# Four column tiles of 32 in place of two of 64 for the values and the probability products of a decoder's self and cross attention

## The chip, the cores and the metric

The kernel runs on one core of a Trainium2 chip. The metric is the device time of one execution in microseconds; the kernel before takes 1644.26 us, the median of three runs (1642.93 to 1644.7). All times of the profile are microseconds from the start of the span unless ns is written. Engines: TensorE has two rows in a profile, PE for matmuls and PEld for the loads of stationary operands; VectorE is DVE, ScalarE is ACT, GpSimd is POOL, SyncE (which issues DMAs) is SP.

## The reference, cut to what matters

Two decoder layers over x and a context, both of shape (64, 64, 128), fp32: 64 sequences of 64 tokens. The change lies in the first two of six steps, a self and a cross attention with 16 heads of 8 dimensions. Cut to its core, with x the tokens that ask and kv the tokens that are read (x itself, then the context):

```python
q, k, v = x @ Wq, kv @ Wk, kv @ Wv          # 128 -> 16 heads of 8
s = einsum('bhnd,bhmd->bhnm', q, k) / sqrt(8)   # cross: causal mask
attn = softmax(s, axis=-1)
out = einsum('bhnm,bhmd->bhnd', attn, v)
x = layernorm(x + (out @ Wo + b))
```

After them come a feed-forward layer, a differential attention, a latent attention with routing, and a mixture of experts. They are untouched by the change.

## The kernel before, in words

**Tiling.** The 64 sequences are taken in 32 pairs, so that 128 tokens fill the partitions. Self attention over the 32 pairs and cross attention over the same 32 run as one pipeline of 64 items in the class `LowHeads`. Each engine has its own method (`tensor`, `scalar`, `vector`, `gpsimd`, `sync`), and each of them is a list of slots: slot i does a piece of item i and pieces of its neighbours. `slots` writes slots -1 to 7 out, then runs a loop of five iterations of four slots (`Fori(2, 7)`), writes 28 to 35 out, runs six iterations of four slots (`Fori(9, 15)`), and writes the rest out. The flags in the code mean: `on(d)`, item i + d exists; `cr(d)`, it is a cross item.

**One slot of TensorE** (the order is written out by hand; every engine takes its instructions in program order, and the engines meet only at semaphores):
- `scores(i)`, L342: eight matmuls for item i, each with 32 rows (four heads) and 64 stationary columns (queries of one sequence); the keys, spread by head on the diagonal (`k_diag`), move, 256 columns. It waits for `qT_ready`, `kd_ready` and `sub_done`: the score banks must have been read. A cross item adds mask matmuls in bf16 (L353).
- L379: transposes of the tokens of item i + 1.
- `turn(i, par, 0)`, L366: four transposes of the probabilities of item i - 1, heads 0 to 7.
- L388: transpose of the normed output of item i - 2.
- L397: keys of item i + 1. Then `turn(.., 1)`, the other four transposes. L403: the output projection of item i - 2. L408: queries of item i + 1.
- L414, the values of item i + 1: the stationary operand is the tokens of one sequence (64 columns), the moving one the value weights of the even or of the odd heads (`wv`, 128 columns with zeros between). Even heads land in partitions 0 to 63 of the bank, odd ones in 64 to 127. Four matmuls.
- L428, the products of the probabilities with the values, item i - 1: for each of 8 pairs of heads and each of 2 sequences, 64 queries are the stationary columns; 18 columns move (8 + 8 values and two columns of ones for the sums of the probabilities). Sixteen matmuls. Afterwards `av_done` rises.

An fp32 matmul shows in the trace as two passes, each with its own load and matmul record (a transpose as one); so L414 has 8 records a slot and L428 has 32.

**The other engines.** VectorE takes, for item i, the maximum of the scores of heads 0 to 7 (L515) and subtracts it (L520, which raises `sub_done`), and the same for heads 8 to 15; between the two it adds the output projection of item i - 2 to z (L554, waits for L403), afterwards it takes the statistics of z (L559). At the start of the slot it takes the reciprocal of the sums (L530, waits for `av_done`) and norms the output (L538). ScalarE copies tokens (L452), the transposed output (L458), keys (L463), transposed probabilities (L469, twice), queries (L474) and values (L484, waits for `av_done`), and takes the exponentials (L444, twice). GpSimd spreads the keys (L599, 1.04 us) and does the rest of the norm. SyncE issues the loads and stores.

**PSUM.** The values lie in bank 2, which holds a half of the transposed probabilities at another time of the slot; the products lie in bank 1.

Of the kernel before, what the change touches and what calls it, by code (L numbers as in the profile page):

```python
# [29 lines left out]
P = 128  # L30
B, S, D = 64, 64, 128
# [14 lines left out]
def wait(eng, sem, count):  # L46

    if not isinstance(count, int) or count > 0:
        eng.wait_ge(sem, count)
# [145 lines left out]
class LowHeads:  # L195
# [121 lines left out]
    def tensor(self, pe, between=None):  # L317
        core, nc = self.core, self.nc
        ps_qk, ps_tail = core.bank[0], core.bank[1]
        ps_t = [core.bank[2], core.bank[3]]  # L320
        ps_v, ps_x = ps_t[0], ps_t[1]
        ps_s = [core.bank[4 + g] for g in range(4)]
        ps_o = ps_tail[:, 0:VW * H0 // 2].rearrange("p (g e) -> p g e", e=VW)
        ps_oT, ps_out = ps_tail[:, 2 * P:3 * P], ps_tail[:, 3 * P:4 * P]

        def cross_weights():

            pe.wait_ge(self.loads[1].loaded, self.loads[1].all)
            for n in range(4):
                last = nc.tensor.transpose(ps_tail[:, n * P:(n + 1) * P], self.loads[1].tile["raw"][:, n, :],  # L330
                                           core.ident[:, :])
            last.then_inc(self.flat_done, 1)

        def scores(i, par, cross):

            wait(pe, self.qT_ready, i + 1)
            wait(pe, self.kd_ready, i + 1)
            wait(pe, self.sub_done, 2 * i)
            for g in range(4):
                at = slice(32 * g, 32 * (g + 1))  # L340
                for b in range(2):
                    last = nc.tensor.matmul(  # L342
                        ps_s[g][b * S:(b + 1) * S, 0:4 * S].rearrange("p (h t) -> p h t", h=4),
                        self.qT[at, par, b * S:(b + 1) * S], self.k_diag[at, par, :, b * S:(b + 1) * S],
                        start=True, stop=not cross)
                if not cross and g % 2:
                    last.then_inc(self.s_done, 1)
            if cross:
                for half in range(2):
                    for g in range(4):  # L350
                        at = slice(32 * g, 32 * (g + 1))
                        cols = slice(half * S // 2, (half + 1) * S // 2)
                        last = nc.tensor.matmul(  # L353
                            ps_s[g][:, 0:4 * S].rearrange("p (h t) -> p h t", h=4)[:, :, cols],
                            self.masks.left[at, half, :, :, :].rearrange("p b f l -> p (b f l)"),
                            self.masks.right[at, half, None, :].to_broadcast([S // 2, 4, S // 2]), start=False,
                            stop=half == 1)
                        if half and g % 2:
                            last.then_inc(self.s_done, 1)

        def turn(i, par, c):

            wait(pe, self.exp_done, 2 * i - 1 + c)
            for hp in range(4):
                src = self.prob[:, 1 - par, 8 * c + 2 * hp:8 * c + 2 * hp + 2, :].rearrange("p h t -> p (h t)")
                last = nc.tensor.transpose(ps_t[c][:, hp * P:(hp + 1) * P], src, core.ident[:, :])  # L366
            last.then_inc(self.t_done, 1)

        def slot(i, k, par, on, cr):
            if on(0):  # L370
                scores(i, par, cr(0))
            if on(1):

                cross = cr(1)
                wait(pe, self.x_loaded[1 - par], 32 * (k + par + 1) - 8 * NPAIR if cross else 16 * (k + par + 1))
                wait(pe, self.pT_ready, 2 * i - 2)
                wait(pe, self.xT_ready, i + 1)
                for m in range(2 if cross else 1):
                    last = nc.tensor.transpose(ps_x[:, m * P:(m + 1) * P], self.x_t[:, 1 - par, m, :], core.ident[:, :])  # L379
                last.then_inc(self.xt_done, 1)  # L380
            if on(-1):

                wait(pe, self.v_ready, i + 1 if on(0) else NI)
                turn(i, par, 0)
            if on(-2):

                wait(pe, self.onorm_done, i - 1)
                nc.tensor.transpose(ps_oT, self.o_norm[:, par, :], core.ident[:, :]).then_inc(self.ot_done, 1)  # L388
            if on(1):

                w = int(cr(1))
                if isinstance(i, int) and i == -1:
                    pe.wait_ge(self.w_copied, 5)
                wait(pe, self.xT_ready, i + 2)
                wait(pe, self.qT_ready, i + 1)
                kv = self.xT[:, w, :]
                nc.tensor.matmul(ps_qk[:, P:2 * P], self.wk[:, w, :], kv, start=True, stop=True).then_inc(self.k_done, 1)  # L397
            if on(-1):
                turn(i, par, 1)
            if on(-2):  # L400

                wait(pe, self.oT_ready, i - 1)
                nc.tensor.matmul(ps_out, self.oT[:, :], self.wo[:, int(cr(-2)), :], start=True, stop=True)\  # L403
                    .then_inc(self.out_done, 1)
            if on(1):

                wait(pe, self.kT_ready, i + 2)
                nc.tensor.matmul(ps_qk[:, 0:P], self.wq[:, w, :], self.xT[:, 0, :], start=True, stop=True)\  # L408
                    .then_inc(self.q_done, 1)

                wait(pe, self.pT_ready, 2 * i - 1)
                for b in range(2):
                    for odd in range(2):
                        last = nc.tensor.matmul(ps_v[odd * S:(odd + 1) * S, b * P:(b + 1) * P],  # L414
                                                kv[:, b * S:(b + 1) * S], self.wv[:, w, odd, :], start=True, stop=True)
                last.then_inc(self.v_done, 1)
            if isinstance(i, int) and i == -1:
                cross_weights()
            if on(-1):

                wait(pe, self.z_done, i - 1)
                if isinstance(i, int) and i == 1:
                    pe.wait_ge(self.w_copied, 10)
                for hp in range(8):
                    if hp % 4 == 0:
                        wait(pe, self.pT_ready, 2 * i - 1 + hp // 4)
                    for b in range(2):
                        last = nc.tensor.matmul(ps_o[b * S:(b + 1) * S, hp, :], self.probT[:, hp, b * S:(b + 1) * S],  # L428
                                                self.v_blk[:, 1 - par, b, hp, :], start=True, stop=True)
                last.then_inc(self.av_done, 1)  # L430

        pe.wait_ge(self.consts.ident_done, 1)
        self.slots(pe, slot, between)

    def scalar(self, act, between=None):
# [2188 lines left out]
```

## Time and profile before

| | us |
|---|---|
| median of the runs (1642.93, 1644.26, 1644.7) | 1644.26 |
| span of the profiled execution | 1642.7 |
| PE busy | 1577.1 (96%) |
| PEld busy | 1321.5 (80%) |
| DVE busy | 1227.7 (75%) |
| ACT busy | 914.9 (56%) |
| POOL busy | 676.4 (41%) |

The profiled execution's own time is given by its span alone; the lowest run, 1642.93, lies 0.2 above it and the median 1.6. Busy times of PE are sums over overlapping, modelled matmuls: an engine that shows work at each moment need not be the limit. What a line of a timeline means: start, length from the first start to the last end of merged instructions, engine, line of the code, operation, tile written and tiles read, shape, number, and in brackets the idle time of the engine before it with what ended it. A shape as 128*64 128x18 is that of a matmul: 128 rows and 64 columns of the stationary operand, 18 moving columns. "Granted clock" (PEclk) is the TensorE clock that the throttle let through, as a share of 2.4 GHz.

### The profile page before, as it was taken

To read this page: it belongs to the slowest core of one execution; us is meant where nothing else is said; L and a number is where in the kernel's file an instruction comes from. 1 tells how busy PE (TensorE), PEld (TensorE's weight loads), DVE (VectorE), ACT (ScalarE), POOL (GpSimd) and SP (SyncE) were. 2 spreads that over 40 slices of the span, in tenths; PEclk is the share of its full clock that TensorE was granted. 3 is DMA by queue.
4 is the path that set the end of the run, shared out by engine and by line. 5 is a ranking of instruction groups with operands and counts; after the bars stand their busy time and mean duration, and the time that the engine had idled before them with its cause. 6 is when DMAs were issued, how large, how long until landed. Compare 5 with 4: busy or idle time off the path is not lost. (4 is left out here: it accounts for less than half of the span.)

```text
span 1642.7 us, 51985 instructions
## 1 busy us (share of the span) xinstructions
PE 1577.1 (96%) x18084; PEld 1321.5 (80%) x18084; DVE 1227.7 (75%) x3513; ACT 914.9 (56%) x2620; POOL 676.4 (41%) x1068
## 2 busy tenths in 40 slices
PE   7999999999999999999999999899999999999795
PEld 5887788787777777777777777699999999999664
DVE  6889888677776777777777677478888888888664
ACT  5777777643544445544444545566666666666251
POOL 3666665411233333333333333234444444444345
PEclk9999999999999999999999999999999999999997
DMA  3214212121221000000001010122122122122231
GB/s 98 74 44 120 72 56 58 44 58 46 61 58 27 26 26 26 26 26 26 26 26 29 27 30 22 30 58 63 44 63 61 43 63 61 44 63 59 77 116 32
DMA packets 157654, 82.30 MB, mean 50 GB/s; under 512 B 17641, under 2 KB 153115, under 8 KB 157568
## 3 DMA queue, kind: packets, MB, share of 16 engines
q1 hardware_dynamic: 154800, 77.68, 17.7%
q0 software_dynamic: 2048, 3.15, 0.6%
q8 instruction: 52, 0.85, 0.2%
q10 hardware_dynamic: 720, 0.33, 0.1%
q14 instruction: 34, 0.28, 0.1%
HBM read 61.03 MB, written 21.27 MB: 50 GB/s over the span
## 5 line engine op out<-in xcount | busy, mean ns | idle before, releaser
L1489 PE MATMUL bank<-diff_xT,diff_w_score 128*128 128x128 f32 x2048 | 256.4, 278 | 0.7 <-ACT diff_xT L1606 0.7
L1489 PEld LDWEIGHTS bank<-diff_xT,diff_w_score 128*128 128x128 f32 x2048 | 238.7, 192 | 22.4 <-issue 20.2
L1613 ACT ACTIVATE diff_keys<-bank 128x512 f32<-128x512 f32 x256 | 152.3, 595 | 161.7 <-PE bank L1489 161.7
L2092 ACT ACTIVATE lat_prob<-bank,lat_neg_max 128x128 f32<-128x128 f32 x512 | 180.7, 367 | 89.9 <-DVE lat_neg_max L2247 89.4
L1803 POOL TENSOR_TENSOR diff_prob<-diff_prob,diff_inv_sum 128x512 f32<-128x512 f32 x64 | 67.1, 1049 | 369.4 <-DVE diff_inv_sum L1706 369.4
L2309 POOL TENSOR_TENSOR lat_prob<-lat_prob,lat_inv_sum 128x512 f32<-128x512 f32 x128 | 133.4, 1042 | 147.6 <-DVE lat_inv_sum L2229 146.6
L1983 PE MATMUL bank<-lat_catT,lat_w_score 128*128 128x128 f32 x1024 | 137.9, 278 | 3.2 <-issue 2.6
L2015 PE MATMUL bank<-lat_catT,lat_query 128*128 128x128 f32 x1024 | 138.7, 278 | 2.3 <-ACT lat_query L2103 2.1
L2003 PE MATMUL bank<-lat_w_vo,lat_ctxT 128*128 128x128 f32 x1024 | 130.3, 275 | 1.1 <-ACT lat_ctxT L2115 1.1
L1983 PEld LDWEIGHTS bank<-lat_catT,lat_w_score 128*128 128x128 f32 x1024 | 124.4, 192 | 4.8 <-issue 3.9
L2015 PEld LDWEIGHTS bank<-lat_catT,lat_query 128*128 128x128 f32 x1024 | 124.5, 192 | 4.7 <-ACT lat_query L2103 3.7
L2003 PEld LDWEIGHTS bank<-lat_w_vo,lat_ctxT 128*128 128x128 f32 x1024 | 122.1, 192 | 1.3 <-ACT lat_ctxT L2115 1.3
L1993 PE MATMUL bank<-lat_probT,lat_c_rep 32*128 32x256 f32 x2048 | 119.5, 380 | 2.4 <-DVE lat_z L2217 2.4
L1993 PEld LDWEIGHTS bank<-lat_probT,lat_c_rep 32*128 32x128 f32 x2048 | 102.0, 185 | 11.0 <-issue 2.6
L2103 ACT ACTIVATE lat_query<-bank 128x512 f32<-128x512 f32 x128 | 76.7, 599 | 57.5 <-PE bank L1983 56.8
L599 POOL TENSOR_TENSOR low_k_diag<-low_kT,low_head_of 128x512 f32<-128x512 f32 x64 | 66.5, 1040 | 100.0 <-ACT low_kT L463 100.0
L1517 PE MATMUL bank<-diff_mix,diff_raw_qkv 128*64 128x128 f32 x1024 | 105.1, 278 | 1.0 <-DVE diff_mix L1732 1.0
L2223 DVE STREAM_TRANSPOSE lat_probT<-lat_prob 128x512 f32<-128x512 f32 x128 | 90.8, 709 | 19.5 <-POOL lat_prob L2309 12.0
L2092 ACT ACTIVATION_READ_ACCUMULATOR lat_prob<-bank,lat_neg_max 128x1 f32 x512 | 104.9, 205 | 0.0
L1766 DVE STREAM_TRANSPOSE diff_probT<-diff_prob 128x768 f32<-128x768 f32 x64 | 62.6, 979 | 56.4 <-POOL diff_prob L1807 54.7
L1517 PE MATMUL bank<-diff_mix,diff_wv 128*64 128x128 f32 x1024 | 102.7, 273 | 0.0
L1732 DVE COPY diff_mix<-bank 128x512 f32<-128x512 f32 x128 | 82.5, 686 | 24.2 <-PE bank L1504 24.2
(274 smaller groups left out, 3684.3 us busy)
## 6 DMA issues: line engine op xcount, KB each, us to landing
lat_c_rep<-cat SPq DMA_DIRECT2D x128, 128.0 KB
stage<-low_y SPq DMA_DIRECT2D x64, 64.0 KB, 1.6
diff_x_rep<-stage SPq DMA_DIRECT2D x128, 32.0 KB, 1.8
lat_c_t<-cat SPq DMA_DIRECT2D x32, 128.0 KB, 2.2
exp_w<-in_L_ffn_w_dram SPq DMA_DIRECT2D x16, 256.0 KB
expert_rows<-latw_zeros SPq DMA_DIRECT2D x4, 548.0 KB, 5.6
exp_rows<-expert_rows SPq DMA_DIRECT2D x8, 274.0 KB
low_x_t<-in_x_dram SPq DMA_DIRECT2D x32, 64.0 KB, 1.9
```

Of the source, the lines that this page charges most:

```text
L1489: last = nc.tensor.matmul(ring[(k + d) % 2][:, j * P:(j + 1) * P], w_score[:, H1 * (k // 2) + HS * d + 4 * (k % 2) + j, :], xT[:, :], star ...
L1517: last = nc.tensor.matmul(ring[d][par * HD1:(par + 1) * HD1, t * P:(t + 1) * P] .rearrange("p (b f l) -> p b f l", b=2, f=2), w, tokens, s ...
L1613: nc.scalar.activation(keys[:, k // 2, 4 * (k % 2):4 * (k % 2) + 4, :].rearrange("p h t -> p (h t)"), ring[(k + d) % 2][:, :], ACT.Copy).t ...
L1732: nc.vector.tensor_copy(mix[:, q % 2::2, :, q // 2, :], ps_mix[q][:, :].rearrange("p (f h l) -> p f h l", f=2, h=HS))\
L1983: last = nc.tensor.matmul(ps_g[:, h * P:(h + 1) * P].rearrange("p (b s) -> p b s", b=2), w_score[:, 4 * c + h, :], catT[:, par, :, S:T], s ...
L1993: last = nc.tensor.matmul(ps_c[r][:, 256 * b:256 * (b + 1)].rearrange("p (c h s) -> p c h s", c=4, h=2), c_rep[at, b, tq, :], moving, star ...
L2003: last = nc.tensor.matmul(ps_o, ctxT[:, 2 * m + odd, :, :].rearrange("p b s -> p (b s)"), w_vo[:, odd, m, :], start=(n == 0), stop=(n == 15))
L2015: last = nc.tensor.matmul(ps[:, m * T:(m + 1) * T], query[:, c % 2, b, 2 * hp:2 * hp + 2, :].rearrange("p h s -> p (h s)"), catT[:, par, b ...
L2092: last = nc.scalar.activation(prob[:, q, m, :], ps_s[q][:, m * T:(m + 1) * T], ACT.Exp, bias=neg_max[:, q, m:m + 1], accum_out=row_sum[:, ...
L2103: nc.scalar.activation(query[:, c % 2, :, :, :], ps_g[:, :].rearrange("p (h b s) -> p b h s", h=4, b=2), ACT.Copy)\
L2223: nc.vector.transpose(probT[:, par if c > 1 else 1 - par, (c + 2) % 4, :, :] .rearrange("p m t -> p (m t)"), prob[:, q, :, :].rearrange("p ...
L2309: nc.gpsimd.tensor_tensor(prob[:, q, :, :], prob[:, q, :, :], inv_sum[:, q, :, None].to_broadcast([P, 4, T]), ALU.mult)\
```

## The change

The values of a sequence were one matmul for each of even and odd heads, with 64 stationary columns (its tokens); they become two with 32 columns, each on a column tile of 32. The products of a pair of heads were one matmul for each sequence, with 64 stationary columns (its queries); they become two with 32 columns. What lands in which partition of the bank is the same, as are the waits, the semaphores and the work of the other engines. L is 32.

```diff
@@ tensor()
+        L = S // 2
@@ values
                 for b in range(2):
-                    for odd in range(2):
-                        last = nc.tensor.matmul(ps_v[odd * S:(odd + 1) * S, b * P:(b + 1) * P],
-                                                kv[:, b * S:(b + 1) * S], self.wv[:, w, odd, :], start=True, stop=True)
+                    for n in range(4):
+                        odd, at = n // 2, b * S + L * (n % 2)
+                        last = nc.tensor.matmul(ps_v[L * n:L * (n + 1), b * P:(b + 1) * P], kv[:, at:at + L],
+                                                self.wv[:, w, odd, :], start=True, stop=True)
@@ products
-                    for b in range(2):
-                        last = nc.tensor.matmul(ps_o[b * S:(b + 1) * S, hp, :], self.probT[:, hp, b * S:(b + 1) * S],
-                                                self.v_blk[:, 1 - par, b, hp, :], start=True, stop=True)
+                    for n in range(4):
+                        at = slice(L * n, L * (n + 1))
+                        last = nc.tensor.matmul(ps_o[at, hp, :], self.probT[:, hp, at], self.v_blk[:, 1 - par, n // 2, hp, :],
+                                                start=True, stop=True)
```

## Rows read from the trace of the kernel before

**Rows 1.** Windows: stretch and length; busy us and records of PE, PEld, DVE, ACT, POOL; clock; DMA.
```profile
66.00:133.00 67.00, 67.00 (x1122) 55.68 (x1120) 58.41 (x160) 52.36 (x142) 43.69 (x79) 1.00 0.16 46
...
194.00:287.00 93.00, 92.97 (x1598) 74.79 (x1583) 75.19 (x198) 69.42 (x180) 55.17 (x99) 1.00 0.20 56
```
**Rows 2.** Timeline of an ordinary self slot, 104.4 to 109.6.
```profile
104.48 0.22 PE L428 MATMUL bank<-low_v_blk,low_probT 128*64 128x18 f32 x2
...
104.65 0.69 PE L342 MATMUL bank<-low_k_diag,low_qT 32*64 32x256 f32 x16
...
105.63 0.28 ACT L452 ACTIVATE low_xT<-bank 128x128 f32<-128x128 f32 x1
...
107.22 0.29 DVE L554 TENSOR_TENSOR low_z<-low_z,bank 128x128 f32<-128x128 f32 x1 [0.28 <-PE bank L403]
...
107.39 0.66 PE L414 MATMUL bank<-low_wv,low_xT 128*64 128x128 f32 x8
...
107.88 1.06 PE L428 MATMUL bank<-low_v_blk,low_probT 128*64 128x18 f32 x32
...
108.14 0.69 DVE L520 TENSOR_TENSOR low_prob<-bank,low_row_max 128x512 f32<-128x512 f32 x1
...
108.89 0.69 PE L342 MATMUL bank<-low_k_diag,low_qT 32*64 32x256 f32 x16
109.05 0.39 ACT L484 ACTIVATE low_v_blk<-bank 128x256 f32<-128x256 f32 x1 [0.54 <-PE bank L428]
```
**Rows 3.** Timeline, the first slot that has products, 21.5 to 23.6.
```profile
22.04 1.06 PE L428 MATMUL bank<-low_v_blk,low_probT 128*64 128x18 f32 x32
23.03 0.69 PE L342 MATMUL bank<-low_k_diag,low_qT 32*64 32x256 f32 x16
...
23.15 0.26 DVE L530 RECIPROCAL low_inv_sum<-bank 128x16 f32<-128x16 f32 x1 [1.67 <-PE bank L428]
```
**Rows 4.** Timeline, a cross slot, 235 to 241.
```profile
235.13 1.06 PE L428 MATMUL bank<-low_v_blk,low_probT 128*64 128x18 f32 x32
...
235.40 0.69 DVE L520 TENSOR_TENSOR low_prob<-bank,low_row_max 128x512 f32<-128x512 f32 x1
...
236.15 0.69 PE L342 MATMUL bank<-low_k_diag,low_qT 32*64 32x256 f32 x16
...
240.83 0.69 PE L342 MATMUL bank<-low_k_diag,low_qT 32*64 32x256 f32 x16
```
**Rows 5.** Timelines of PE and PEld near 1335: a matmul with 8 moving columns.
```profile
1335.56 0.29 PE L2040 MATMUL bank<-lat_router,lat_yT 128*128 128x8 f32 x2
...
1335.45 0.30 PEld L2040 LDWEIGHTS bank<-lat_router,lat_yT 128*128 128x128 f32 x2
1335.67 0.41 PEld L2015 LDWEIGHTS bank<-lat_catT,lat_query 128*128 128x128 f32 x3
```
**Rows 6.** Timelines of PEld and PE near 711.5: four column tiles of 32.
```profile
711.49 0.16 PEld L1529 LDWEIGHTS bank<-diff_keys,diff_xT 128*32 128x32 f32 x8 [0.17 <-issue]
...
711.50 0.64 PE L1529 MATMUL bank<-diff_keys,diff_xT 128*32 128x512 f32 x4
...
711.50 1.06 PE L1529 MATMUL bank<-diff_keys,diff_xT 128*32 128x512 f32 x8
```
**Rows 7.** Timeline, the last slot that has products, near 310.
```profile
310.23 0.26 DVE L530 RECIPROCAL low_inv_sum<-bank 128x16 f32<-128x16 f32 x1 [0.96 <-PE bank L428]
```
**Rows 8.** Timeline, the self slot at a loop's back edge, 99.5 to 101.8.
```profile
100.33 0.69 PE L342 MATMUL bank<-low_k_diag,low_qT 32*64 32x256 f32 x16
...
101.39 0.28 ACT L452 ACTIVATE low_xT<-bank 128x128 f32<-128x128 f32 x1
```
**Rows 9.** Window of one later loop iteration; DMA queues and issues of 560 to 920.
```profile
544.00:583.60 39.60, 39.60 (x429) 30.70 (x428) 28.11 (x66) 19.42 (x38) 13.34 (x23) 1.00 0.10 27
...
q1 hardware_dynamic: 21888, 9.45, 9.7%
...
low_x_t<-in_x_dram SPq DMA_DIRECT2D x32, 64.0 KB, 1.9
```

## Prediction

> **What bounds the kernel now.** I first read which stage the change touches, then one slot of it in order of time, and asked of each wait which event ended last. The touched lines run in the first 310 us: the self slots (66 to 133 us holds the loop), the cross slots (loop in 194 to 287 us), and unrolled slots around them. In both windows TensorE shows work at every moment, its granted clock is 1.00, and VectorE is busy for 87 and 81% [rows 1]. That makes TensorE look like the bound, but matmuls overlap, so the slot must be followed event by event.
>
> One ordinary self slot runs from one score block (L342, 104.65) to the next (108.89), 4.24 us [rows 2]. Two chains lead to its end. VectorE's: the output projection L403 releases z (L554, 107.22), then a maximum, then the subtraction L520 at 108.14 for 0.69, which ends at 108.83; the scores start 0.06 later. TensorE's: values (L414) from 107.39, products (L428) from 107.88. Their 32 passes cover 1.06, one pass being 0.21 (the row at 104.48 has two in 0.22), so the last one starts at 107.88 + 1.06 - 0.21 = 108.73; the scores start 0.16 later. Which ends last? At the start of the kernel the scores (23.03) follow the last product pass (22.04 + 1.06 - 0.21 = 22.89) by 0.14, with VectorE idle since long [rows 3]. So 0.14 is what TensorE needs to get from products to scores. The ordinary slot has 0.16: TensorE would be ready some 0.02 earlier, and the subtraction ends last. The cross slot gives the same pair of distances: L520 ends at 235.40 + 0.69 = 236.09, the last product pass starts at 235.98, the scores at 236.15 [rows 4]. The products are thus almost, but not quite, on the path; the two chains are nearly tied.
>
> **The change part by part.** *Products (L428).* A slot has 16 matmuls of two passes, x32 [rows 2]; it gets 32 matmuls, 64 passes, each with 32 stationary columns in place of 64 and the same 18 moving columns. Each of the four column tiles gets as many passes, 16, as each of the two has now. What sets the time of such a pass? The 32 passes with 64 columns start (1.06 - 0.21)/31 = 0.027 apart, 0.055 to 0.06 on one tile [rows 2]. A matmul with 8 moving but 128 stationary columns shows two loads in the 0.22 before the next group's: 0.11 each [rows 5]. So with few moving columns the time follows the stationary ones: 128 give 0.11, 64 give under 0.06. By that halving I estimate 0.032 for 32. Can four tiles be fed so fast? Eight loads of 32 columns, for four column tiles, cover 0.16 at 0.11 each, so they start (0.16 - 0.11)/7 = 0.007 apart, and a round of four needs only 0.03 [rows 6]. The products then run from first to last start in 15 x 0.032 + 3 x 0.007 = 0.50 in place of 0.85: 0.35 earlier. Bounds: rounds of 0.028 (four loads at 0.007) give 0.44; rounds as long as now give 0.02 more than now, from the wider round, which the spare 0.02 takes up.
>
> *Values (L414).* x8 a slot [rows 2] becomes 16. Here 128 columns move, and four rounds on two tiles take 107.88 - 107.39 = 0.49 up to the first product. Each tile keeps four passes of 128 moving columns, and four column tiles work side by side: four passes of 512 moving columns cover 0.64, eight 1.06 [rows 6], so a round of four takes 0.42, and a quarter of the columns 0.105. So four rounds stay four rounds: no gain, and 0.01 later for the last tile. The bounds are 0 and the price of rival C. The other engines keep their instructions; no wait is added and no queue is passed.
>
> *Where 0.35 a slot goes.* In an ordinary slot nothing that ends last waits for the products. The next scores wait for L520, which hangs on L403, issued before the products. The reciprocal (L530) stands in VectorE's order behind L520. Only ScalarE's copy of the values (L484, 109.05) waits for the products, 0.54 idle [rows 2]; it would start earlier, but the exponential behind it needs L520's result, and the token copy L452 behind that needs transposes that follow the scores. So I cost it at nothing in these slots; what is late next is L520. The cover is VectorE's chain from 107.22 to 108.83; without it the change would be worth 0.35 in each slot, some 22 us.
>
> *Where it counts.* (1) The first slot with products, where the scores stand straight behind them [rows 3]: -0.35. (2) The last slot: VectorE idles 0.96 until they end [rows 7], and all up to the feed-forward layer follows: -0.35. (3) The slot at a loop's back edge: it lasts 104.65 - 100.33 = 4.32, 0.08 more than 4.24. There ScalarE's L452 comes 1.06 behind the scores (100.33 to 101.39), in the ordinary slot 0.98 (104.65 to 105.63) [rows 2, 8]. ScalarE's branch lies between L484 and L452; with L484 done earlier it falls into idle time, and I expect the 0.08 back. The loops have 5 and 6 iterations of four slots, so 4 + 5 = 9 back edges: -0.7 (bounds 0 and -0.7).
>
> **Sum** against the profiled execution: 1642.7 - 0.35 - 0.35 - 0.7 = 1641.3 of span. The median of the runs, 1644.26, lies 1.6 above the profiled span, so I predict 1642.8, 0.1% less. 0.2%, 3.3 us, is about what a measurement of this kernel can tell from no change.
>
> **Rivals.** *A, each pass has a floor (slower).* Then the doubled number costs. If no pass can start sooner than 0.025 after the one before, 64 passes take 63 x 0.025 = 1.58 in place of 0.85: 0.73 more, less 0.02 spare, in some 62 slots: +44, 1688. The floor decides from (0.85 + 0.02)/63 = 0.014 a pass on. Against it: the starts 0.007 apart [rows 6]. For it: that row has eight passes in a row, not 64; a queue may feed eight fast and 64 not. Chance 0.08. Such a floor is a rule of the Trainium skill: "TensorE: Matmul & The Clock Gate", section "Wait — 56ns, not 53.3ns?", says that starts never get closer than about 25 ns however few columns move, and "TensorEngine Tiling (Array Packing)", section "Instruction Overhead", gives each matmul some 60 cycles of overhead. By these rules the change is the wrong one; the trace does not agree for tiles side by side, with its 0.007.
>
> *B, a loop no longer stays loaded (slower).* The loop of the later stage takes 429 matmuls in its 39.6 us and fetches no instruction while it runs: its DMA list has the data queue alone [rows 9]. The self loop would have 1122/67 x 17.0 + 160 = 445 and the cross loop 1598/93 x 18.7 + 160 = 481 passes an iteration (four slots last 17.0 and, at 240.83 - 236.15 = 4.68 each, 18.7) [rows 1, 4], more than that row covers. If each of 9 back edges waited for one transfer of 1.9 (what 64 KB take to land), it is +17: 1660. Chance 0.03.
>
> *C, the values block or the switch between tile shapes gets dearer (slower).* If the products start 0.05 to 0.2 later and their rounds don't win it back, 0.03 to 0.18 in 62 slots is +2 to +11: 1646 to 1655. It decides once the block from values to products loses more than 0.02. No row shows 128 x 32 tiles beside 128 x 128 and 32 x 64 in this stage. Chance 0.13, of it 0.09 beyond 3.3 us.
>
> *D, the rounds don't get shorter (no change).* A round could be a fixed part that the columns don't touch: 1644. Chance 0.08.
>
> *E, the products are on the path after all (faster).* If the tie of the two chains is misread, or ScalarE's earlier copy pulls L452 forward in every slot, up to 0.1 in each of 62 slots comes free besides: 1637. For it: L452 starts as soon as ScalarE's exponential is through. Against: in the cross slot the same 0.16 and 0.06 stand though ScalarE's work differs. Chance 0.10.
>
> **How the numbers follow.** Forecast 0.58 (1641 to 1644.5), D 0.08, E 0.10, C 0.13, A 0.08, B 0.03. Slower by over 0.2%: A, B and most of C, 0.20; faster: E, 0.10; within: the rest, 0.70. The range from 1639 to 1652 leaves out A, B, the deep end of E and the top of C, a little under 0.2.
>
> **What would show it.** The product passes should take 0.50 from first to last start, the values still 0.49 up to the first product. The scores should still start 0.06 behind the end of L520, and the last product pass some 0.5 before them; ordinary slots stay at 4.24 and 4.68, the back-edge slot falls from 4.32 to about 4.24. The granted clock stays at 1.00 with TensorE's busy time down by up to 0.35 a slot. I am wrong if the product passes stand 0.014 or more apart (A), if instruction transfers appear in the loops (B), if the ordinary slot grows (C) or shrinks (E) by more than 0.02.

## The result and the profile after

The changed kernel takes 1648.95 us (median of 20 executions, 1643.86 to 1653.24) where the kernel before takes 1644.35 beside it (20 executions, 1642.26 to 1651.97): a ratio of 1.0021, 95% interval 1.0011 to 1.0031. So it is slower, by about 3.4 us by the ratio, where a tenth of a per cent less was forecast. The range held the time, the direction was wrong. All executions of this study were in the fast state but one, of the run with TensorE's loop cut elsewhere (3071.74 us), which is left out.

In the changed kernel some lines move: the scores are L343 (L342 before), the values L416 (L414), the products L431 (L428), the subtraction that releases the scores L523 (L520), the copy of the values L487 (L484), the token copy L455 (L452), z L557 (L554). An ordinary self slot of the profile after, from score block to score block (answers to [rows 2]):

```profile
92.08 0.69 PE L343 MATMUL bank<-low_k_diag,low_qT 32*64 32x256 f32 x16 [0.28 <-DVE low_prob L523]
...
94.65 0.29 DVE L557 TENSOR_TENSOR low_z<-low_z,bank 128x128 f32<-128x128 f32 x1 [0.29 <-PE bank L404]
94.82 0.38 PEld L416 LDWEIGHTS bank<-low_wv,low_xT 128*32 128x32 f32 x16 [0.19 <-ACT low_probT L472]
...
95.28 0.76 PE L431 MATMUL bank<-low_v_blk,low_probT 128*32 128x18 f32 x64
...
95.58 0.69 DVE L523 TENSOR_TENSOR low_prob<-bank,low_row_max 128x512 f32<-128x512 f32 x1
...
96.15 0.39 ACT L487 ACTIVATE low_v_blk<-bank 128x256 f32<-128x256 f32 x1 [0.21 <-PE bank L431]
...
96.32 0.24 PEld L343 LDWEIGHTS bank<-low_k_diag,low_qT 32*64 32x64 f32 x16 [0.38 <-DVE low_prob L523]
```

The slot still lasts 96.32 - 92.08 = 4.24. One product pass lasts 0.184 in the mean (the grouped rows of L431), so the 64 of them start within 0.76 - 0.18 = 0.58, that is 0.009 apart, and the last one starts at 95.86. The scores come 0.46 later, 0.05 after the subtraction has ended (95.58 + 0.69 = 96.27). TensorE now waits visibly for VectorE, "0.28 <-DVE low_prob L523", where before it was busy without a gap. The windows say the same, 62.00 busy in place of 67.00 [rows 1], at the same granted clock:

```profile
66.00:133.00 67.00, 62.00 (x1710) 50.24 (x1710) 57.87 (x156) 52.29 (x140) 42.81 (x77) 1.00 0.16 45
194.00:287.00 93.00, 86.62 (x2410) 67.75 (x2402) 75.21 (x198) 68.71 (x177) 55.37 (x100) 1.00 0.20 55
```

So the products got shorter and the ordinary slots did not care. What got longer shows in two other places. The first is the slot at a loop's back edge (answers to [rows 8]):

```profile
99.52 0.76 PE L431 MATMUL bank<-low_v_blk,low_probT 128*32 128x18 f32 x64
...
99.82 0.69 DVE L523 TENSOR_TENSOR low_prob<-bank,low_row_max 128x512 f32<-128x512 f32 x1
...
100.39 0.39 ACT L487 ACTIVATE low_v_blk<-bank 128x256 f32<-128x256 f32 x1 [0.21 <-PE bank L431]
...
100.74 0.69 PE L343 MATMUL bank<-low_k_diag,low_qT 32*64 32x256 f32 x16 [0.46 <-DVE low_prob L523]
...
101.81 0.28 ACT L455 ACTIVATE low_xT<-bank 128x128 f32<-128x128 f32 x1 [0.52 <-PE bank L380]
```

The subtraction ends at 100.51, and the scores start 0.23 later, not 0.05. The branch of TensorE stands between the products and these scores. This slot, the last of its iteration, lasts 100.74 - 96.32 = 4.42. In what follows "back edge" means this slot. Three of the four of the self loop last 4.39 to 4.42 where they lasted 4.24 to 4.25, the first 4.47 (4.28 before); the five of the cross loop 4.82 where they lasted 4.74 (the first) and 4.68. It is not the slot that the prediction called by that name, the first of an iteration: that one took 4.32 before and takes 105.07 - 100.74 = 4.33 here.

```profile
105.07 0.69 PE L343 MATMUL bank<-low_k_diag,low_qT 32*64 32x256 f32 x16 [0.28 <-DVE low_prob L523]
```

The second is inside blocks of products in the slots that are written out, outside the loops. TensorE stops in the middle of a block and waits for nothing but its own next instruction ("issue"):

```profile
158.30 0.55 PEld L431 LDWEIGHTS bank<-low_v_blk,low_probT 128*32 128x32 f32 x38
...
158.40 0.54 PE L431 MATMUL bank<-low_v_blk,low_probT 128*32 128x18 f32 x38
...
160.84 0.33 PEld L431 LDWEIGHTS bank<-low_v_blk,low_probT 128*32 128x32 f32 x26 [2.00 <-issue]
160.84 0.43 PE L431 MATMUL bank<-low_v_blk,low_probT 128*32 128x18 f32 x26 [1.90 <-issue]
```

38 of the 64 products, a hole of 1.9 us, then the other 26. There are four such holes, as the list of TensorE's waits from 25 to 310 us says (us in total, times, the longest); the list of the kernel before has no such line:

```profile
PE bank L343 <- DVE low_prob L523: 20.4, 57, 1.2
...
PE bank L431 <- issue: 3.2, 4, 1.9
```

The list of DMA queues shows why TensorE could run out of instructions: the transfers that fetch code rose from 52 (0.85 MB) to 61, 16 KB each.

```profile
q8 instruction: 61, 1.00, 0.3%
```

To add these up I use one measure for all kernels below: the **stretch** from the third score block (the first that follows products) to the last one of the cross part, worked out from the starts of the blocks' first loads. It is 279.13 us before and 283.18 after, +4.05: the nine back edges make +1.3 (0.14 to 0.17 each, but 0.19 and 0.09 for the first of either loop), the holes and late instructions in written-out slots and at the loops' entries the rest (slot 12, the first of the second iteration, takes 0.31 more, slot 7 takes 5.05 in place of 4.27, slot 5 4.69 in place of 4.34, slots 32 and 33 together 11.36 in place of 10.33; slots are counted from 0). The span grew by only 2.4 (1642.7 to 1645.1), because the third score block comes 1.4 earlier (21.59 in place of 23.03). Most of that is no merit of the change: the profile before had a stretch at a granted clock of 0.5, at 14.6 to 21.4 us, that the profile after has not. The first slot with products did gain: from the start of the values to the scores it took 23.03 - 21.55 = 1.48, and takes 1.14, both at full clock.

```profile
20.45 0.64 PE L416 MATMUL bank<-low_wv,low_xT 128*32 128x128 f32 x16
20.91 0.76 PE L431 MATMUL bank<-low_v_blk,low_probT 128*32 128x18 f32 x64
21.59 0.69 PE L343 MATMUL bank<-low_k_diag,low_qT 32*64 32x256 f32 x16
```

The last one gained too (answer to [rows 7]): VectorE waits 0.58 in place of 0.96 for the last products, and from the last score block to the reciprocal it is 7.66 in place of 8.03. Behind the last score block the kernel is 0.18 shorter in all (1340.31 in place of 1340.49).

```profile
312.46 0.26 DVE L533 RECIPROCAL low_inv_sum<-bank 128x16 f32<-128x16 f32 x1 [0.58 <-PE bank L431]
```

One more thing is needed to read the medians. The mean granted clock of a whole execution varies, and the time with it, by 1.0 to 1.3 us for each 0.001 in the executions of these two kernels. At 0.990 or more, the changed kernel has a median of 1646.93 (12 of 20 executions) against 1644.54 (51 of 56 executions of the kernel before, in the first two sets of experiments): +2.4, as the spans say. For the 20 of the kernel before in the comparison itself no clocks are recorded; 5 of them took 1647.85 or more, which in the 91 executions of that kernel beside the experiments only those at 0.989 or less did. So it may well have been 8 of 20 against 5 of 20, and the medians above carry some of that chance.

### The profile page after: what moved, and what is told of

The parts are those of the page before. It is cut to its first block and busy times, and to the rows that moved or that the text cites. A ratio compares the mean times of both kernels' runs of the same rounds, so it can differ in the third digit from the quotient of the medians.

```text
span 1645.1 us, 57105 instructions
## 1 busy us (share of the span) xinstructions
PE 1559.6 (95%) x20644; PEld 1301.3 (79%) x20644; DVE 1227.5 (75%) x3513; ACT 916.7 (56%) x2620; POOL 676.9 (41%) x1068
```

## The experiments

**Theory** after the comparison: the tiles are worth nothing in a slot whose end VectorE sets; their cost is in TensorE's instructions, twice as many: they reach the branch later, and in straight code they run dry. **Rivals:** a cost in every slot, from the switch between tile shapes or the values (C of the prediction); or something about the start and the stage changes that is not tied to the instructions.

### The change in the loops alone

```diff
-                    for n in range(4):
-                        at = slice(L * n, L * (n + 1))
...
+                    if isinstance(i, int):
+                        for b in range(2):
...
+                    else:
+                        for n in range(4):
+                            at = slice(L * n, L * (n + 1))
```

The two-tile form of before stands under the condition, and the same is done for the values; i is an integer in the written-out slots only.

> The change only in the 44 slots inside the two loops, the old form in the slots that are written out. Theory 1 (the loss has two parts: in the written-out slots TensorE runs out of instructions inside the product blocks, some 2.9 us over six slots, and each of nine back edges is 0.14 to 0.16 longer, 1.3 us): no pause over 0.3 us in any product block or at a loop's entry, back-edge slots still 4.40 and 4.82 where they were 4.24 and 4.68, the run 1 to 1.5 us above the kernel before (ratio 1.001). Rival (the narrow tiles themselves or the switch between tile shapes cost): the ordinary loop slots grow, or the whole loss of 3.4 us stays though only the loops have the new form.

Median 1650.38 (9 executions), ratio 1.0033 (1.0015 to 1.0051), above the 1.001 that was expected, but 6 of the 9 had a mean granted clock of 0.989 or less; the times alone don't decide between theory and rival, the trace does. The profiled execution had 0.993 and a span of 1641.2 (its profile lacks the stretches at half clock near 15 and 315 us that the one before has). In it no block of products has a hole, ordinary slots stay at 4.24 and 4.68, the back edges take 4.40 to 4.43 and 4.82 to 4.85, and the stretch is 280.42: 1.29 more than before, where the nine back edges add up to 1.35. The holes and late instructions, 2.8 us of the stretch, therefore come from the new form in the written-out slots, and the back edges account for the rest.

```profile
98.18 0.76 PE L442 MATMUL bank<-low_v_blk,low_probT 128*32 128x18 f32 x64
...
99.05 0.39 ACT L498 ACTIVATE low_v_blk<-bank 128x256 f32<-128x256 f32 x1 [0.21 <-PE bank L442]
...
99.38 0.69 PE L343 MATMUL bank<-low_k_diag,low_qT 32*64 32x256 f32 x16 [0.44 <-DVE low_prob L534]
```

### The products alone, and the values alone

The first run is the changed kernel with the values taken back:

```diff
-                    for n in range(4):
-                        odd, at = n // 2, b * S + L * (n % 2)
...
+                    for odd in range(2):
```

The second has the products taken back instead:

```diff
-                    for n in range(4):
-                        at = slice(L * n, L * (n + 1))
...
+                    for b in range(2):
```

> Products on four column tiles, values on two as before: 64 more PE records a slot in place of 80. Theory 1 (number of instructions): pauses and back edges shrink a little, in the ratio of the added instructions, some 0.12 a back edge; run +2.7 us. Rival (the values on four tiles bring the loss): run as before within 0.5 us.

1646.32 (12 executions), ratio 1.0018 (1.0005 to 1.0030), stretch 282.10. Ordinary slots 4.24 and 4.68, but back edges of 4.49 to 4.54 and 4.93 to 4.98, about 0.26 more than before, twice the loss of the whole change and twice the 0.12 that was expected.

> Values on four column tiles, products on two as before: 16 more PE records a slot. Theory 1: no pause in a product block, back edges at most 0.03 longer, product block later by 0.02; run within 1 us of before. Rival (the values bring the loss): +3 us.

1652.21 (7 executions), ratio 1.0058 (1.0038 to 1.0079), stretch 283.99. It was expected within 1 us of the kernel before; the rival was right. Here every ordinary slot grew, to 4.36 and 4.79. One slot of each, first the products alone, then the values alone:

```profile
94.53 0.66 PE L415 MATMUL bank<-low_wv,low_xT 128*64 128x128 f32 x8
...
95.12 0.74 PE L430 MATMUL bank<-low_v_blk,low_probT 128*32 128x18 f32 x64
95.29 0.69 DVE L522 TENSOR_TENSOR low_prob<-bank,low_row_max 128x512 f32<-128x512 f32 x1
...
96.03 0.69 PE L343 MATMUL bank<-low_k_diag,low_qT 32*64 32x256 f32 x16 [0.17 <-DVE low_prob L522]
```
```profile
96.28 0.64 PE L416 MATMUL bank<-low_wv,low_xT 128*32 128x128 f32 x16
...
96.85 1.11 PE L430 MATMUL bank<-low_v_blk,low_probT 128*64 128x18 f32 x32
97.03 0.69 DVE L522 TENSOR_TENSOR low_prob<-bank,low_row_max 128x512 f32<-128x512 f32 x1
...
97.90 0.69 PE L343 MATMUL bank<-low_k_diag,low_qT 32*64 32x256 f32 x16
...
98.07 0.39 ACT L486 ACTIVATE low_v_blk<-bank 128x256 f32<-128x256 f32 x1 [0.68 <-PE bank L430]
```

From the start of the values to the products it is 0.59 and 0.57 when the two have different tiles, 0.49 when both have tiles of 64 [rows 2], 0.46 when both have tiles of 32. With different tiles the loads of the products also start after an idle time of 0.17 and 0.20 that the traces with equal tiles don't have. So a switch between the tile widths costs TensorE about 0.1. That is rival C, and the trace agrees here with the Trainium skill ("TensorEngine Tiling (Array Packing)", section "Key Properties"), by which a change of the tiling mode makes the engine drain. In the products alone the 0.1 is hidden (the scores start 0.05 after the subtraction has ended at 95.98) except at the back edges, where it comes on top. In the values alone the subtraction ends at 97.72 and the scores start 0.18 later with no wait for it: the products, started 0.09 later and 0.05 longer (1.11 in place of 1.06), now set the slot. This confirms how little the two chains were apart before. The full change switches nowhere between values and products, so it escapes C: its two halves belong together.

### TensorE's loop cut elsewhere

Here `blocks` holds the values and products, taken out of `slot`. Each iteration of TensorE's loops now begins with those of the slot before, so that no branch stands between products and scores.

```diff
             with pe.Fori(first // 4, end // 4) as q:
                 for m in range(4):
+                    blocks(4 * q + m - 1, 2 * q + (m - 1) // 2, (m - 1) % 2, lambda d: True, lambda d: cross)
                     slot(4 * q + m, 2 * q + m // 2, m % 2, lambda d: True, lambda d: cross)
```

> The change, with TensorE's loop cut at another place of the slot: the branch stands between the queries (L408 of before) and the values, where TensorE waits 0.2 us for ScalarE anyway, and no longer behind the products. Theory 1: the scores follow the subtraction by 0.06 at the back edge too, so nine slots lose their 0.15, and the run is 1.3 us below the changed kernel, +2 us over before; the pauses in written-out slots stay (they may move to other slots). Rival (the 0.15 comes from something else at the back edge, ScalarE's or VectorE's own branch): slots of 4.40 and 4.82 stay.

1645.9 (11 executions), ratio 1.0008 (0.9997 to 1.0019). All nine back edges are back at 4.24 to 4.25 and 4.68, so the branch's place is their cause. The first slots of the iterations stay at 4.32 and 4.76. The largest hole stayed, and at the same place: 1.6 us from 158.61 on in the products of slot 32, with slots 32 and 33 at 6.35 and 6.70 (a stretch at half clock from 161.8 on lengthened slot 33); slot 9 took 4.91.

```profile
99.53 0.76 PE L436 MATMUL bank<-low_v_blk,low_probT 128*32 128x18 f32 x64
...
100.40 0.39 ACT L509 ACTIVATE low_v_blk<-bank 128x256 f32<-128x256 f32 x1 [0.21 <-PE bank L436]
...
100.57 0.69 PE L343 MATMUL bank<-low_k_diag,low_qT 32*64 32x256 f32 x16 [0.28 <-DVE low_prob L545]
```

What the branch costs is put best from the last product pass. Five traces have four-tile products ahead of the branch: those of the changed kernel, of the change in the loops alone, of the products alone, and the two with an early projection and uncut loops that follow below. In them the scores behind a back edge start 0.61 to 0.70 after the start of the last product pass, in 44 of 45 cases (the other: 0.74), whether the subtraction ended 0.2 or 0.5 before them. In the three with two-tile products there it is 0.16 to 0.22, in all 27. So the branch sets a point that is fixed to the products, not an addition to the slot, and the earlier VectorE is, the more it costs.

### Moving VectorE's chain

If VectorE's chain sets the slot, moving it up must release what the products gained, and must release next to nothing before the change. The output projection, from which the chain starts, is issued after two of the slot's four later transposes in place of all four.

```diff
             for hp in range(4):
+                if hp == 2 and between:
+                    between()
...
             if on(-1):
-                turn(i, par, 1)
-            if on(-2):
...
+                turn(i, par, 1, project if on(-2) else None)
```

> The kernel before, with the output projection (L403) issued after the first two of the four transposes of the slot, so that VectorE's L554, L520 and with them the scores may start earlier. Theory (in the kernel before, the products chain ends at most 0.02 us ahead of the point from which it would set the slot, as the run with only the values changed showed: 4.36 us per slot once the products ended 0.1 later): the slot stays at 4.22 to 4.24 us self and 4.66 to 4.68 cross, the total at 0 to -1.3 us. Rival (products have spare time already, and VectorE's chain alone sets the slot): slots of about 4.05 us, total about -12 us.

1645.51 (12 executions), ratio 1.0010 (0.9997 to 1.0024). Its slots went to 4.22 and 4.66, by 0.02 each, and no further:

```profile
111.26 1.06 PE L432 MATMUL bank<-low_v_blk,low_probT 128*64 128x18 f32 x32
...
111.41 0.69 DVE L524 TENSOR_TENSOR low_prob<-bank,low_row_max 128x512 f32<-128x512 f32 x1
...
112.26 0.69 PE L342 MATMUL bank<-low_k_diag,low_qT 32*64 32x256 f32 x16
```

The subtraction ends at 112.10, the scores start 0.16 later: now TensorE's products are last. The 0.02 of the prediction was right. The stretch fell to 276.45, by 2.7, more than the 1.3 that was allowed: in the slots written out, which took 4.33 and 4.77 before, 0.11 and 0.19 were to be had. The median did not fall; 10 of the 12 executions had a mean clock of 0.989 or less, though all of this kernel's matmuls have the old form. The other two took 1642.49 and 1644.01, against 1644.7 (27) beside them.

> The changed kernel with the same edit: the output projection after two of the four transposes. Theory (the change made the products end about 0.4 us earlier, which is worth nothing only because VectorE's chain from the output projection ends last): the chain moved up by some 0.2 us now moves the scores up with it, slots of 4.05 to 4.15 us in the loops against 4.24, back-edge slots about 0.15 above that as before, total -6 to -12 us against the kernel before. Rival (the slot is bound by something else behind it, TensorE's own order or ScalarE's L414 and L452): slots stay at 4.24 and the total at +2 to +3 us.

1643.82 (12 executions), ratio 0.9990 (0.9977 to 1.0002); so no more than level with the kernel before, where 6 to 12 us less were expected; at a clock of 0.990 or more 1640.74 (6), 4.0 less. Ordinary slots 4.13 and 4.46, by 0.11 and 0.22 shorter than in either kernel, but back edges 0.3 and 0.4 above them in place of the expected 0.15 (4.42 to 4.43 after a first of 4.71, and 4.87 to 4.95), slot 9 at 5.04, and a hole of 1.6 us from 158.64 on once more.

```profile
109.59 0.69 PE L343 MATMUL bank<-low_k_diag,low_qT 32*64 32x256 f32 x16 [0.17 <-DVE low_prob L527]
...
112.79 0.76 PE L435 MATMUL bank<-low_v_blk,low_probT 128*32 128x18 f32 x64
...
112.97 0.69 DVE L527 TENSOR_TENSOR low_prob<-bank,low_row_max 128x512 f32<-128x512 f32 x1
...
113.72 0.69 PE L343 MATMUL bank<-low_k_diag,low_qT 32*64 32x256 f32 x16 [0.17 <-DVE low_prob L527]
```

> As the run with the changed kernel and the early output projection, but with the values left on two column tiles of 64. Theory: the values are off the path, so the loop slots equal those of the run with both parts within 0.1 us (the products start 0.1 later, with 0.3 to 0.4 to spare), the back edges cost 0.1 more each, total within 2 us of that run. Rival (the product block counts once VectorE's chain is earlier): slots 0.1 us longer than with both parts, total some 6 us above it.

1640.62 (12 executions), ratio 0.9982 (0.9972 to 0.9992), faster than the kernel before. Slots as in the run before within 0.01, stretch 275.28 against 276.23: the products alone carry the gain, and with fewer instructions the largest hole is 0.5 us. The expected two microseconds between the runs were 3.2 in the medians, 0.5 at a clock of 0.990 or more.

> The run before this one with TensorE's loops cut between the queries and the values, so that the products of a slot and the scores that follow lie in one iteration. Theory: back-edge slots equal the other loop slots within 0.03 us, total 1 to 2.5 us below the run before this one; with both edits the kernel is 6 to 13 us below the kernel before. Rival (the branch only moves its cost to the values): the back-edge slots stay 0.15 to 0.25 above the others and the total is the same within 1 us.

1638.81 (5 executions), ratio 0.9963 (0.9950 to 0.9976), stretch 271.94. The back edges fell from about 4.5 to 4.13 to 4.16 in the self loop, and from 4.93 to 4.98 to 4.56 to 4.67 in the cross loop, where their neighbours have 4.47 and 4.55; in the cross loop 0.09 is thus left, where 0.03 was expected. It is 3.3 us of the stretch, more than the 1 to 2.5 expected, because a back edge cost 0.35 to 0.45 once the chain was earlier.

### Straight code everywhere

Both kernels with their loops written out on all engines.

```diff
-        with eng.Fori(2, NPAIR // 4 - 1) as q:
-            for m in range(4):
-                slot(4 * q + m, 2 * q + m // 2, m % 2, lambda d: True, lambda d: False)
+        for i in range(8, NPAIR - 4):
+            slot(i, i // 2, i % 2, lambda d: True, lambda d: False)
```

> The kernel before with its loops written out on every engine (44 more slots of straight code, the same work in the same order). Instruction theory: TensorE's code is fetched in pieces of 16 KB, one for every 7.4 us of this kernel's slots, and one piece is usable 2.4 to 2.8 us after its transfer begins, so that the supply keeps up: few holes, ordinary slots 4.24 and 4.68, stage longer by 0 to 4 us. Rival (the holes come from straight code as such, not from its density): the written-out slots lose as much as in the next run.

1645.89 (10 executions), ratio 1.0013 (1.0001 to 1.0025), stretch 281.33. No hole, but all slots take 4.33 and 4.77, 0.09 more than in a loop. The excess lies between the end of the subtraction and the scores, 0.15 in place of 0.05, and stands in both kernels of this pair; its cause was not followed further.

> The changed kernel with its loops written out in the same way. Instruction theory: a slot holds half as many TensorE instructions again, 16 KB go in some 4.5 us, and the holes that the changed kernel shows in its written-out slots (0.06, 0.35, 0.78, 0.19, 0.31 us in slots 5, 6, 7, 11, 12, about 0.25 a slot of slots 4 to 12) now come in the 44 slots of the old loops too, less the nine back edges (1.3 us): 5 to 20 us above the run before this one, with holes of 0.4 to 2 us inside the blocks of products and values. Rival (the holes belong to the start and the two stage changes, where other code is new as well): within 2 us of the run before this one.

1646.76 (10 executions), ratio 1.0023 (1.0012 to 1.0033), stretch 282.97. That is 1.6 above the run before it by the stretch, not 5 to 20: the theory of density failed, and the outcome is that of its rival. In the self part TensorE's code arrives every 4.9 us here in place of every 7.4, and nearly all slots stay at 4.33 and 4.77. There is one large hole, in slot 7:

```profile
43.34 0.64 PE L429 MATMUL bank<-low_v_blk,low_probT 128*32 128x18 f32 x51
...
44.50 0.31 PE L429 MATMUL bank<-low_v_blk,low_probT 128*32 128x18 f32 x13 [0.52 <-issue]
```

Slots 6, 7, 9, 28, 46, 47 and 48 are longer by 0.1 to 0.4. In steady straight code the supply keeps up with twice the product passes.

That the holes are waits for code is shown by when they end. Six profiles have waits for "issue" inside blocks of products, twelve in all (four in the changed kernel). Every one of them ends 1.2 to 1.5 us after a transfer of code has landed, 2.3 to 2.6 after it began, though such transfers come only every 4 to 8 us there. The hole of 1.6 to 1.9 us in slot 32, five slots behind the end of the first loop, is in three kernels that have that loop and four-tile values and products behind it, and is missing here. In the changed kernel the transfers behind that loop begin at 140.0, 145.6, 151.7 and 158.5, then at 162.7 and 167.2; the one at 158.5 began 0.3 us before TensorE stopped, took 1.15, and the products went on 2.4 after its start. So this transfer was no slower than others, it began late, 6.8 us behind the one before. Why, the runs don't tell, and a loop's exit is not the whole of it: of the four holes of the changed kernel two, 0.65 and 0.39 us, lie at 38.24 and 43.01, in slots written out ahead of the first loop.

### Old form outside the loops, new form inside

The fastest run so far (products on four tiles, values on two, early projection, loops cut before the values), with two-tile products in the written-out slots.

> The fastest run so far (products on four tiles, values on two, output projection after two transposes, TensorE's loops cut between queries and values) with the old two-tile products in the written-out slots. Instruction theory: the holes of the written-out slots (0.5 to 1 us each in slots 1, 6, 8, 11 and 36 or so) go, while those slots stay at 4.22 instead of 4.13; total 0 to 2 us below that run, 6 to 8 us below the kernel before. Rival (the holes are not tied to the number of instructions): the same holes, total 0.5 to 1 us above it.

1634.76 (5 executions, 1634.50 to 1635.02) against 1643.61 for the kernel before beside it: ratio 0.9947 (0.9932 to 0.9962), a gain of 0.5% and the best of this study. The stretch is 271.32, 0.6 below the run that it was made from, and no block of products has a hole; slot 10 still takes 4.59 in place of 4.24. By the ratios the two runs stand 2.6 apart, in separate sets, a little over the 0 to 2 that were expected. At a clock of 0.990 or more they are 8.0 (5 against 16 executions) and 7.0 (4 against 27) below the kernel before beside them, 1.0 apart: nearer the stretch, and too few executions to say more. Slots 13 to 15 of its self loop, the last of them a back edge, are 4.12 to 4.13 each:

```profile
68.82 0.69 PE L343 MATMUL bank<-low_k_diag,low_qT 32*64 32x256 f32 x16
...
72.94 0.69 PE L343 MATMUL bank<-low_k_diag,low_qT 32*64 32x256 f32 x16
...
77.07 0.69 PE L343 MATMUL bank<-low_k_diag,low_qT 32*64 32x256 f32 x16
...
81.20 0.69 PE L343 MATMUL bank<-low_k_diag,low_qT 32*64 32x256 f32 x16
```

### The change without its costs

The whole change in the looped slots, the loops cut before the values, the projection left where it was.

> The change (values and products) in the looped slots alone, and TensorE's loops cut between queries and values: both costs found so far are taken away (holes in written-out slots, late branch), and the output projection stays after the four transposes. Theory (the tiles themselves are worth nothing while VectorE's chain ends last): ordinary slots 4.24 and 4.68, back edges within 0.03 of them, no hole above 0.2 us in a block of products, runs at a mean granted clock of 0.990 or more within 0.5 us of the kernel before. Rival (the new form costs something besides, in every slot or in contention): 1.5 us or more above it at that clock. The run also shows whether executions with a mean clock of 0.989 or less, 5 of 55 in the kernel before and 8 of 20 in the changed one, stay frequent when the slots keep their old times.

1642.36 (11 executions), ratio 1.0001 (0.9987 to 1.0014); at a clock of 0.990 or more 1642.34 (9) against 1643.06 (12) beside it, just outside the 0.5 that was expected. The stretch is 278.93, before 279.13. No block of products has a hole; slot 9, at the loop's entry, takes 4.62 in place of 4.39, and the back edges take 4.24 to 4.25 and 4.68 to 4.71, within the 0.03 that was expected. So the tiles alone are worth next to nothing, as forecast, and late branches and holes are what they cost. 2 of the 11 executions had a mean clock of 0.989 or less. Over all runs that number goes from 0 of 5 to 10 of 12, and the 10 of 12 are those of a kernel with the old matmuls only, so it is not tied to the new form of matmul as such. Its profiled execution was one of them. The columns are busy time and records of PE, PEld, DVE, ACT and POOL, the granted clock, the DMA share and GB/s; first the kernel before, then this one, behind the end of the cross part:

```profile
307.00:315.00 8.00, 6.45 (x61) 4.05 (x61) 2.76 (x13) 3.55 (x10) 4.09 (x9) 1.00 0.06 17
```
```profile
307.00:315.00 8.00, 6.91 (x54) 4.92 (x52) 2.15 (x10) 2.53 (x7) 2.58 (x6) 0.50 0.07 18
```

A clock of 1.2 in place of 2.4 GHz for some 17 us, from 306.6 on, between the cross part and the next stage, where the kernel before had some 3 us of it, stands in this profile and in that of the kernel before with the early projection. What decides between the two stayed open.

## Why the prediction was wrong, point by point

- *VectorE's chain ends last, the products 0.02 before it.* Right, and shown from both sides: 0.14 of delay (the products 0.09 later and 0.05 longer) lengthened every slot by 0.12, and an earlier chain won 0.02 without the four-tile products and 0.11 to 0.22 with them.
- *The products, 0.85 to 0.50.* The mechanism was right, the size a little off: 0.574 from first to last start. The first 24 passes start 0.0076 apart, a round of four in 0.030, close to the 0.032 that was worked out; the other 40 start 0.010 apart, and rounds of 0.040 were not foreseen. That is a little of what rival A held against the row of eight. Its floor does not exist here, over 64 passes: where "TensorE: Matmul & The Clock Gate" of the Trainium skill puts starts at least 25 ns apart, this trace has 9 ns on four tiles.
- *The values cost nothing.* Right only together with the products (0.46 to the first product); alone they cost 0.12 a slot. Rival C had its mechanism and its price right, and did not apply to the whole change.
- *Nothing in ordinary slots.* Right: 4.24 and 4.68.
- *Nine back edges, -0.08 each, -0.7 in all.* This is the first step that failed, twice over. The 0.08 did not come back: the first slot of an iteration takes 4.33 in place of 4.32, with ScalarE idle for 0.52 ahead of L455, which still comes 1.07 behind the scores. So a busy ScalarE was not its cause. TensorE's branch is not either, since the slot keeps its 4.32 where that branch is moved; the cause is open. And the slot ahead of it grew, by 1.3 us in nine. I did not look at TensorE's own branch, which stands there. Before, it was hidden: at six of the nine back edges the scores came within 0.01 of where the subtraction alone would have put them. Of each step that puts more instructions ahead of a branch I should have asked when the branch is reached.
- *First and last slot, -0.35 each.* Right: -0.34 and -0.37 where the prediction placed them. Of the second 0.18 is left at the end of the kernel. These terms are not missing from the result, they are outweighed by what the sum had no term for.
- *Instruction supply.* Rival B looked for it in the loops alone, where it stayed at nothing: they stay loaded. The written-out slots around them had no term in the sum, without a reason given. This is the second failed step, and the larger one: some 2.7 us of the stretch, of which 0.3 lie in slot 12 of the loop, right behind its first back edge. The 3.2 us of waiting inside four blocks of products are its visible part; some of them fell into time that VectorE set anyway.
- *The range* held by luck: it reached to 1652 for the prices of rivals C and B, and neither is what made the kernel slower.

## What to carry to other kernels

Doubling the number of instructions of an engine is not free because its busy time falls: look at the branch that stands behind the block and at the straight code around the loops, where code has to be fetched while it runs. A block that ends ahead of another chain's end is worth its gain only after that chain has been moved; here moving one matmul up turned a loss of 0.2% into a gain of 0.2% (products alone), and with the two costs taken away one after the other it was 0.5%. Change tile widths in adjacent blocks together or count the switch.

## What the runs showed of the hardware

- Matmuls on four column tiles of 32, with 18 moving columns, start 9 ns apart in the mean over 64 passes; on two tiles of 64 it is 27 ns, in turn 7 and 52.
- A switch between blocks with column tiles of 64 and 32 costs TensorE about 0.1 us, in either direction.
- At a branch of TensorE the matmuls behind it started 0.61 to 0.70 us after the start of the last of 64 product passes, and 0.16 to 0.22 after the last of 32 slower ones. It cost nothing where they had to wait that long anyway, 0.14 to 0.17 a branch in the changed kernel, and 0.3 to 0.4 when the scores could have started earlier.
- TensorE's loops stay loaded: between 66 and 140 us no code was fetched for it, though four slots of the changed kernel are some 59 KB (36 more slots written out took 94 transfers of 16 KB in place of 61) and about 440 matmul passes (1710/67 x 17.0 = 434 in the window, 445 by the prediction's count).
- Straight code came in transfers of 16 KB, every 4.9 us in the mean in the changed kernel with its loops written out. A piece could be used 2.3 to 2.6 us after its transfer began; where TensorE needed it sooner, it stood still, up to 1.9 us in the middle of a block.
